# Cross attention blocks: a later row turn, a spread start, and plain fp32 projections in the first layer

## Chip, cores and metric

One core of one Trainium2 chip. The metric is device time in microseconds of the whole kernel (two transformer layers). TensorE is called PE, VectorE DVE, ScalarE ACT, GpSimd POOL and SyncE SP, as in the profile.

## The reference, cut to what matters

Both layers do self attention, cross attention and a feed forward part. x is (4, 1024, 256) in float32 and the context (4, 77, 192); 16 heads, of width 16 in the first layer ("narrow", its weights fake-quantised) and 64 in the second ("wide"). The change touches the cross attention alone:

```
h    = layernorm(x) * g + b                      # rows of 256
q    = (h @ wq).reshape(b, n, 16, HD)            # HD = 16, then 64
sim  = einsum(q, k) * HD ** -0.5                 # k, v from the 77 context rows
out  = einsum(softmax(sim), v).reshape(b, n, 16 * HD)
x    = x + out @ wo + bo
```

## The kernel before

x stays in SBUF through the whole kernel. Each layer calls `context_kv` (keys and values of the context, stored to DRAM), `norm_project` and `attend_...` (self attention), `cross_block` (L2097), and `feed_forward`. Phases are separated by a barrier.

`cross_block` cuts the 4096 rows into 8 tiles of 512 (TT; TB = 4 blocks of 128) and the 16 heads into 8 pairs: 64 slots n = 8 t + p. Every engine has its own loop over n, written out in full, and runs its instructions strictly in that order; semaphores tie them together. In slot n:

- PE (L2457 on): `score(n)` (waits until DVE has read score n-1), the queries due in this slot (`query`), `values(n - 3)`, a piece of the output projection (`project`, four per tile, in slots 7, 8, 11 and 12 from the tile's start), `flip(n - 2)` (transposes of the probabilities), and, if a later tile is due, `turn` (transposes of the normalised rows, L2465).
- DVE (L2319): maximum and subtraction of score n, sum and reciprocal n - 1, the addition of a projected piece to x, `low_query` and `low_out` (the low parts), then for a later tile the statistics, `turn_rows` (normalised rows xhat, L2322) and `low_rows` (L2331).
- ACT (L2396): exp, `high_query`, `high_out` (evictions rounded to the high part), `scale` (gain and offset of the turned rows, L2399), and the copy of the flipped probabilities.
- POOL (L2275): the reciprocal deviations (`norm_rstd`), the bias added to x, the division of the probabilities; before the loop zeroing of buffers and low parts of both weights.
- SP (L2209): all DMAs. In the narrow block `stack(t)` stores the q of a tile to DRAM and loads it back as three parts stacked on partitions; `score` waits for that (`moved`).

A matmul of near fp32 accuracy is made of three float32r passes: high x high, low x high and high x low, with every operand split into a high part (ACT copy to float32r) and a low part (the rest, DVE or POOL). `turn_of(n)` names the tile whose rows are normalised in slot n. LEAD and TURN_AT set it: narrow (2, 5), so tile t in slot 8 (t - 2) + 5; wide (1, 1), so in slot 8 (t - 1) + 1. Statistics come three slots earlier, POOL's deviations two; PE turns in the same slot as `turn_rows`, ACT scales one slot later, `low_rows` two later. Queries of tile t are due from slot 8 (t - 1) + 1 on (narrow, both) and from 8 t - 2 (wide, one a slot). FIRST, the loop's first n, follows from LEAD and TURN_AT: -6 and -2. PSUM results of `turn`, `query`, `values` and `project` go round four banks in the order that `unit` counts; `clear` waits until the one four before has been evicted (`kind_sem`).

Before the loop, SP loads gains, wq, bias, then contexts (all four in the narrow block, two in the wide), and after the low part of wq is made, wo into the same raw buffer.

Of the kernel before, what the change touches and what calls it, by code (L numbers as in the profile page):

```python
# [12 lines left out]
P = 128  # L13
# [83 lines left out]
class Program:  # L97
# [1999 lines left out]
    def cross_block(self, L, x_sb, ident, g, b, wq, wo, bo):  # L2097
# [10 lines left out]
        LEAD, TURN_AT = (2, 5) if narrow else (1, 1)  # L2108
# [54 lines left out]
        with ExitStack() as st:  # L2163
# [6 lines left out]
            ht = sb("ht", [P, DC, TT])  # L2170
            h = [[sb(f"h_{part}{k}", [P, DC, TT], F32R) for k in two] for part in ("hi", "lo")]
            gam, bet = sb("g", [P, DC]), sb("b", [P, DC])
            wraw = sb("wraw", [P, 2048])
            wqr = [sb("wq_hi", [P, DC, L.dim], F32R), sb("wq_lo", [P, DC, L.dim], F32R)]
            wor = [sb("wo_hi", [P, OCH, D], F32R), sb("wo_lo", [P, OCH, D], F32R)]
# [12 lines left out]
            o = [sb("o_hi", [P, OCH, TT], F32R), sb("o_lo", [P, OCH, TT], F32R)]  # L2188
# [3 lines left out]
            gb_in, w_in, b_in, w_hi, w_lo, zeroed = (sem(s) for s in ("gb_in", "w_in", "b_in", "w_hi", "w_lo", "zeroed"))  # L2192
# [11 lines left out]
            ZERO = KVB * 2  # L2204
            WOL = 16 * (G if narrow else 1)
            kind_sem = dict(tp=hh_done, q=q_lo, acc=o_lo, y=y_done)

            @block.sync
            def _(sp):  # L2209
# [24 lines left out]
                raw = wraw[:, 0:DC * L.dim].rearrange("p (c n) -> p c n", c=DC)  # L2234
                sp.dma_start(raw, wq.rearrange("(c p) n -> p c n", p=P)).then_inc(w_in, 16)
                sp.dma_start(bias[:, :], bo.partition_broadcast(P)).then_inc(b_in, 16)
                for bt in range(KVB):
                    sp.wait_ge(zeroed, 2 * bt + 2)
                    context(bt)
                sp.wait_ge(w_lo, 1)  # L2240
                if narrow:
                    sp.wait_ge(zeroed, ZERO + 1)
                    raw = wraw[:, 0:OCH * D].rearrange("p (c n) -> p c n", c=OCH)
                    view = wo.rearrange("(c h e) n -> h e c n", h=G, e=HD)
                    for x in range(G):
                        sp.dma_start(raw[W * x:W * x + HD, :, :], view[x]).then_inc(w_in, 16)
                else:
                    raw = wraw[:, 0:OCH * D].rearrange("p (c n) -> p c n", c=OCH)
                    sp.dma_start(raw, wo.rearrange("(c p) n -> p c n", p=P)).then_inc(w_in, 16)
# [25 lines left out]
            def _(pool):  # L2275
# [14 lines left out]
                size = DC * L.dim  # L2290
                pool.wait_ge(w_hi, 1)
                lo, hi = (wqr[x][:, :, :].rearrange("p c n -> p (c n)") for x in (1, 0))
                g_.tensor_tensor(lo, wraw[:, 0:size], hi.bitcast(F32), ALU.subtract).then_inc(w_lo, 1)
                for k in range(1, KVB):
                    zero(k)
                if narrow:
                    pool.wait_ge(w_lo, 1)
                    g_.memset(wraw[:, 0:OCH * D], 0.0).then_inc(zeroed, 1)
                pool.wait_ge(w_hi, 2)
                lo, hi = (wor[x][:, :, :].rearrange("p c n -> p (c n)") for x in (1, 0))  # L2300
                g_.tensor_tensor(lo, wraw[:, 0:OCH * D], hi.bitcast(F32), ALU.subtract).then_inc(w_lo, 1)
                pool.wait_ge(b_in, 16)
                for n in range(FIRST, SLOTS):
# [5 lines left out]
                    if p == 0:  # L2309
                        pool.wait_ge(n_["chain"], (t + 1) * self.STATS_STEPS)  # L2310
                        xt = x_sb[:, t * TB:(t + 1) * TB, :]
                        g_.tensor_tensor(xt, xt, bias[:, :].unsqueeze(1).broadcast_to((P, TB, D)), ALU.add).then_inc(biased, 1)
# [3 lines left out]
                                     .broadcast_to((P, 2 * TB, M)), ALU.mult).then_inc(p_norm, 1)  # L2316

            @block.vector
            def _(dve):  # L2319
# [42 lines left out]
                low_rows(0)  # L2362
                for c in range(QCH if narrow else 2):
                    low_query(0, c)
                for n in range(FIRST, LAST):
# [20 lines left out]
                    if acc_of(n - 3):  # L2386
# [5 lines left out]
                    if turn_of(n - 2):  # L2392
                        low_rows(turn_of(n - 2))

            @block.scalar
            def _(act):  # L2396
                a_ = nc.scalar

                def scale(t):  # L2399
                    for c in range(DC):  # L2400
                        act.wait_ge(r_ready, at["tp", t, c] + 1)
                    if t > 0:
                        act.wait_ge(hl_done, t)
                    for c in range(DC):
                        a_.activation(ht[:, c, :], bank[at["tp", t, c] % 4][:, :], ACT.Identity, bias=bet[:, c:c + 1],
                                      scale=gam[:, c:c + 1]).then_inc(ht_done, 1)
# [24 lines left out]
                act.wait_ge(w_in, 16)  # L2431
                a_.activation(wqr[0][:, :, :].rearrange("p c n -> p (c n)"), wraw[:, 0:DC * L.dim], ACT.Copy).then_inc(w_hi, 1)
# [3 lines left out]
                act.wait_ge(w_in, 16 + WOL)  # L2436
                a_.activation(wor[0][:, :, :].rearrange("p c n -> p (c n)"), wraw[:, 0:OCH * D], ACT.Copy).then_inc(w_hi, 1)
# [346 lines left out]
```

## Time and profile before

| | us |
|---|---|
| median of 3 runs (lowest, highest) | 4611.16 (4599.38, 4611.64) |
| profiled execution, its own time | 4588.91 |
| its span | 4586.7 |
| PE busy | 4023.8 (88%) |
| DVE busy | 3057.8 (67%) |
| ACT busy | 1795.5 (39%) |
| POOL busy | 1774.3 (39%) |

The spans are those of one execution; busy times are shares of it over all phases. A matmul's duration holds its latency, so the distance from one start to the next tells its price. Clock is the TensorE clock that was granted, as a share of 2.4 GHz; its lower level is 0.5.

### The profile page before, as it was taken

The numbers are of one execution on the slowest core, as the hardware profiler recorded it, in microseconds if no ns is written. First come the engines' busy times: TensorE is split into PE (matmuls) and PEld (weight loads), VectorE is DVE, ScalarE is ACT, GpSimd is POOL, SyncE is SP. The second block draws the span as 40 slices with busy tenths as digits, with TensorE's granted clock in tenths as the row PEclk, the third lists the DMA queues.
The fourth block names the chain that finished last, engine by engine and source line by source line (L and its number), as shares of the span: only waits on it lengthen the run. The fifth ranks groups of instructions, "written<-read, shape, count | busy, mean of one in ns | idle before, by whom it ended". The sixth has DMA issues, their size and how long they took to land. (4 is left out here: it accounts for less than half of the span.)

```text
span 4586.7 us, 67259 instructions
## 1 busy us (share of the span) xinstructions
PE 4023.8 (88%) x25111; PEld 2701.5 (59%) x25111; DVE 3057.8 (67%) x4993; ACT 1795.5 (39%) x2644; POOL 1774.3 (39%) x1164
## 2 busy tenths in 40 slices
PE   0779999995787897699899999999999979999798
PEld 0633333332565676477566666666666647777677
DVE  6768888882676655477567666666666646665565
ACT  0226676764444332111233333333333324444332
POOL 0168800001333000100377877787787762222000
PEclk9859999998788999799799999999999989889899
DMA  4453443421432000577411111111121110000100
GB/s 117 168 88 53 61 40 34 47 20 35 72 62 44 20 0 20 165 279 283 144 70 47 68 49 57 60 48 69 47 70 47 47 37 1 9 9 1 34 15 18
DMA packets 303482, 293.18 MB, mean 64 GB/s; under 512 B 132340, under 2 KB 222612, under 8 KB 302924
## 3 DMA queue, kind: packets, MB, share of 16 engines
q1 hardware_dynamic: 300620, 281.27, 24.0%
q0 software_dynamic: 2560, 7.88, 0.6%
q8 instruction: 191, 3.13, 0.3%
q14 instruction: 111, 0.91, 0.1%
HBM read 160.74 MB, written 127.28 MB: 63 GB/s over the span
## 5 line engine op out<-in xcount | busy, mean ns | idle before, releaser
L1704 POOL TENSOR_TENSOR f_sums<-f_sums,f_probs 128x1024 f32<-128x1024 f32 x384 | 914.3, 2381 | 156.0 <-ACT f_probs L1823 118.1
L1721 DVE TENSOR_REDUCE f_mx<-f_s 128x1 f32<-128x512 f32 x1024 | 660.0, 687 | 383.8 <-PE f_s L1846 372.5
L1823 ACT ACTIVATE f_probs<-f_st 128x1024 f32<-128x1024 f32 x512 | 525.1, 1027 | 939.7 <-PE f_st L1869 935.3
L1327 DVE TENSOR_REDUCE f_mx<-f_s 128x1 f32<-128x512 f32 x1024 | 633.4, 683 | 94.7 <-PE f_s L1464 83.3
L1440 ACT ACTIVATE f_probs<-f_st 128x512 f32<-128x512 f32 x1024 | 530.2, 603 | 252.1 <-PE f_st L1481 251.0
L1846 PE MATMUL f_s<-f_k,f_q 64*128 64x512 f32 x3072 | 516.0, 415 | 21.7 <-DMA f_k<-k 15.6
L1869 PE MATMUL f_st<-f_q,f_k 64*128 64x512 f32 x3072 | 485.9, 390 | 1.1 <-ACT f_probs L1823 1.0
L1883 PE MATMUL f_acc<-f_probs,f_v 128*64 128x512 f32 x2048 | 465.4, 596 | 0.0
L1846 PEld LDWEIGHTS f_s<-f_k,f_q 64*128 64x128 f32 x3072 | 341.9, 189 | 169.8 <-issue 115.2
L1481 PE MATMUL f_st<-f_q,f_k 50*128 50x512 f32 x1024 | 354.7, 485 | 58.3 <-ACT f_probs L1440 58.2
L1869 PEld LDWEIGHTS f_st<-f_q,f_k 64*128 64x128 f32 x3072 | 367.3, 184 | 25.8 <-ACT f_probs L1823 3.8
L2315 POOL TENSOR_TENSOR f_probs<-f_probs,f_rden 128x616 f32<-128x616 f32 x128 | 160.3, 1253 | 550.3 <-DVE f_rden L2381 550.3
L1481 PEld LDWEIGHTS f_st<-f_q,f_k 50*128 50x128 f32 x1024 | 143.4, 189 | 361.2 <-ACT f_probs L1440 312.0
L1464 PE MATMUL f_s<-f_k,f_q 48*128 48x512 f32 x1024 | 317.7, 459 | 22.9 <-DMA f_k<-k 22.6
L576 POOL TENSOR_TENSOR f_ve<-f_var,f_const 128x4 f32<-128x4 f32 x48 | 9.6, 199 | 788.6 <-DVE f_var L557 788.6
L1883 PEld LDWEIGHTS f_acc<-f_probs,f_v 128*64 128x64 f32 x2048 | 141.5, 137 | 266.2 <-issue 257.2
L1493 PE MATMUL f_acc<-f_probs,f_v 128*32 128x512 f32 x2048 | 281.0, 622 | 0.0
L1744 DVE RECIPROCAL f_rd<-f_s 128x512 f32<-128x512 f32 x64 | 214.9, 3358 | 72.4 <-PE f_s L1892 72.4
L1869 PE MATMUL f_st<-f_m,f_mones 64*128 64x512 f32 x1024 | 248.4, 389 | 0.0
L2369 DVE TENSOR_REDUCE f_mx<-f_s 128x8 f32<-128x616 f32 x128 | 101.9, 796 | 207.3 <-PE f_s L2506 206.6
L2634 DVE SCALAR_TENSOR_TENSOR f_u<-f_pa,f_bias,f_gate 128x512 f32<-128x512 f32 x128 | 96.1, 751 | 213.5 <-PE f_pa L2720 213.4
L2671 ACT ACTIVATE f_gate<-f_pg,f_bias 128x512 f32<-128x512 f32 x128 | 88.0, 687 | 380.7 <-PE f_pg L2712 380.7
(258 smaller groups left out, 8334.0 us busy)
## 6 DMA issues: line engine op xcount, KB each, us to landing
q<-f_stage SPq DMA_DIRECT2D x80, 512.0 KB, 2.8
k<-f_stage SPq DMA_DIRECT2D x80, 512.0 KB, 2.8
f_q<-q SPq DMA_DIRECT2D x32, 1024.0 KB, 5.0
f_k<-k SPq DMA_DIRECT2D x32, 1024.0 KB, 7.4
v<-f_v_stage SPq DMA_DIRECT2D x64, 256.0 KB, 3.1
f_v<-v SPq DMA_DIRECT2D x32, 512.0 KB, 8.5
f_q<-q SPq DMA_DIRECT2D x96, 128.0 KB, 4.3
f_k<-k SPq DMA_DIRECT2D x96, 128.0 KB, 7.0
```

What stands on the lines that cost most here:

```text
L1327: v.tensor_reduce(mx[:, i % 2, c:c + 1], bank[u % 4][:, :], AX_X, ALU.max).then_inc(s_free, 1)
L1440: a_.activation(probs[:, n % NP, e % 2, :], stb[k % 3][:, :], ACT.Exp, scale=L.scale).then_inc(p_ready, 1)
L1464: t.matmul(bank[u % 4][:, :], q[cur][rows, j, qb * P:(qb + 1) * P], k_[cur][rows, j, f * HALF:(f + 1) * HALF], start=True, stop=True, tile ...
L1481: t.matmul(stb[n % 3][:, :], k_[cur][rows, j, c * P:(c + 1) * P], q[cur][rows, j, half * HALF:(half + 1) * HALF], start=True, stop=True, t ...
L1493: ins = t.matmul(acc[W * h:W * h + W, :], vs[cur][:, c, h, :], p, start=c == 0, stop=c == KC - 1, tile_position=(0, W * h))
L1704: g_.tensor_tensor(out, out, probs[:, n % NP, :, :], ALU.add).then_inc(sum_done, 1)
L1721: v.tensor_reduce(mx[:, i % 2, c:c + 1], bank[u % 3][:, :], AX_X, ALU.max).then_inc(s_free, 1)
L1744: v.reciprocal(rd[:, half, :], bank[u % 3][:, :]).then_inc(s_free, 1)
L1823: a_.activation(probs[:, s % NP, :, :], stb[s % 2][:, :, :], ACT.Exp, scale=L.scale).then_inc(p_ready, 1)
L1846: ins = t.matmul(bank[u % 3][:, :], q[cur][rows, a, qb * P:(qb + 1) * P], k_[cur][rows, c, f * HALF:(f + 1) * HALF], start=r == 0, stop=r ...
L1869: ins = t.matmul(stb[s % 2][:, h, :], lhs, rhs, start=r == 0, stop=r == 3, tile_position=(64 * h, 0))
L1883: ins = t.matmul(acc[W * h:W * h + W, :], vs[cur][:, c, h, :], probs[:, s % NP, h, :], start=c == 0, stop=c == KC - 1, tile_position=(0, W ...
```

## The change

`turn` follows `turn_rows` by one slot, and `scale` and `low_rows` follow it; the wide block has LEAD 2 and TURN_AT 4, so tile t's rows are normalised in slot 8 (t - 2) + 4 and turned in the next, and FIRST becomes -7. The narrow block keeps plain fp32 h, wq, o and wo: no high and low parts of these four, one matmul for three. (Its q is still split for `stack`.) wo has a raw buffer and a semaphore of its own. SP issues one context, then wo and the bias; further contexts come between the tiles' stacks (narrow) or after (wide). POOL zeroes later context buffers in slots 1 to 3, makes wo's low part in slot 3 (wide), and adds the bias in slot 4 of a tile, not 0.

```diff
-        LEAD, TURN_AT = (2, 5) if narrow else (1, 1)
+        LEAD, TURN_AT = 2, 5 if narrow else 4
...
-            if turn_of(n):
+            if turn_of(n - 1):
                 for c in range(DC):
-                    unit("tp", turn_of(n), c)
+                    unit("tp", turn_of(n - 1), c)
...
+            if narrow:
+                h = [[sb(f"h{k}", [P, DC, TT]) for k in two]]
+            else:
+                ht = sb("ht", [P, DC, TT])
+                h = [[sb(f"h_{part}{k}", [P, DC, TT], F32R) for k in two] for part in ("hi", "lo")]
...
+            wraw, oraw = sb("wraw", [P, DC * L.dim]), sb("oraw", [P, OCH * D])
+            if narrow:
+                wqr, wor = [wraw[:, :].rearrange("p (c n) -> p c n", c=DC)], [oraw[:, :].rearrange("p (c n) -> p c n", c=OCH)]
...
-            o = [sb("o_hi", [P, OCH, TT], F32R), sb("o_lo", [P, OCH, TT], F32R)]
+            o = [sb("o", [P, OCH, TT])] if narrow else [sb("o_hi", [P, OCH, TT], F32R), sb("o_lo", [P, OCH, TT], F32R)]
...
-            kind_sem = dict(tp=hh_done, q=q_lo, acc=o_lo, y=y_done)
+            kind_sem = dict(tp=hh_done, q=q_lo, acc=o_hi if narrow else o_lo, y=y_done)
... SP
-                sp.dma_start(bias[:, :], bo.partition_broadcast(P)).then_inc(b_in, 16)
-                for bt in range(KVB):
-                    sp.wait_ge(zeroed, 2 * bt + 2)
-                    context(bt)
-                sp.wait_ge(w_lo, 1)
+                sp.wait_ge(zeroed, 2)
+                context(0)
+                raw = oraw[:, :].rearrange("p (c n) -> p c n", c=OCH)
                 if narrow:
-                    sp.wait_ge(zeroed, ZERO + 1)
+                    sp.wait_ge(o_zeroed, 1)
...
+                sp.dma_start(bias[:, :], bo.partition_broadcast(P)).then_inc(b_in, 16)
...
                 if narrow:
                     for t in range(TILES):
                         stack(t)
+                        if t + 1 < KVB:
+                            sp.wait_ge(zeroed, 2 * t + 4)
+                            context(t + 1)
                 else:
+                    sp.wait_ge(zeroed, 4)
+                    context(1)
... POOL
-                for k in range(1, KVB):
-                    zero(k)
...
-                    if p == 0:
-                        pool.wait_ge(n_["chain"], (t + 1) * self.STATS_STEPS)
...
                                      .broadcast_to((P, 2 * TB, M)), ALU.mult).then_inc(p_norm, 1)
+                    if 0 < n < KVB:
+                        zero(n)
+                    if n == 3 and not narrow:
+                        pool.wait_ge(w_hi, 2)
+                        lo, hi = (wor[x][:, :, :].rearrange("p c n -> p (c n)") for x in (1, 0))
+                        g_.tensor_tensor(lo, oraw[:, :], hi.bitcast(F32), ALU.subtract).then_inc(w_lo, 1)
+                    if p == 4:
+                        pool.wait_ge(b_in, 16)
+                        pool.wait_ge(n_["chain"], (t + 1) * self.STATS_STEPS)
+                        xt = x_sb[:, t * TB:(t + 1) * TB, :]
+                        g_.tensor_tensor(xt, xt, bias[:, :].unsqueeze(1).broadcast_to((P, TB, D)), ALU.add).then_inc(biased, 1)
... DVE
-                    if acc_of(n - 3):
+                    if acc_of(n - 3) and not narrow:
                         low_out(*acc_of(n - 3))
...
-                    if turn_of(n - 2):
-                        low_rows(turn_of(n - 2))
+                    if turn_of(n - 3) and not narrow:
+                        low_rows(turn_of(n - 3))
... ACT
+                    if n == 2 and not narrow:
+                        act.wait_ge(wo_in, WOL)
+                        a_.activation(wor[0][:, :, :].rearrange("p c n -> p (c n)"), oraw[:, :], ACT.Copy).then_inc(w_hi, 1)
...
-                    if turn_of(n - 1):
-                        scale(turn_of(n - 1))
+                    if turn_of(n - 2):
+                        scale(turn_of(n - 2))
... PE
+                    passes = [(k, 0, 0) for k in range(DC)] if narrow else self.H_PASSES
...
-                    pe.wait_ge(o_lo, nth("acc", t, part * half + half - 1))
-                    pe.wait_ge(w_lo, 2)
+                    pe.wait_ge(kind_sem["acc"], nth("acc", t, part * half + half - 1))
...
-                        work = [(c, x, w) for c in range(part * half, part * half + half) for x, w in ((0, 0), (0, 1), (1, 0))]
+                        work = [(c, x, w) for c in range(part * half, part * half + half) for x, w in (((0, 0),) if narrow else ((0, 0), (0, 1), (1, 0)))]
...
-                    if turn_of(n):
-                        turn(turn_of(n))
+                    if turn_of(n - 1):
+                        turn(turn_of(n - 1))
```

## Rows read from the trace of the kernel before

**Rows 1.** Windows, narrow tiles 0, 1, 6: length, busy PE, PEld, DVE, ACT, POOL; clock
```profile
1155.52:1195.48 39.96, 31.64 (x160) 23.70 (x160) 26.98 (x49) 15.91 (x22) 11.61 (x14) 0.55 0.38 66
1195.48:1236.81 41.33, 33.58 (x228) 26.02 (x228) 30.87 (x57) 19.15 (x27) 15.08 (x16) 0.79 0.39 64
...
1400.83:1431.28 30.45, 25.91 (x220) 19.72 (x220) 25.85 (x43) 16.71 (x23) 11.82 (x10) 1.00 0.53 87
```

**Rows 2.** Windows, wide tiles 0, 3, 6
```profile
3762.91:3816.37 53.46, 43.69 (x335) 33.34 (x336) 34.90 (x60) 22.71 (x32) 19.68 (x23) 0.81 0.01 4
...
3940.67:4002.12 61.45, 59.36 (x441) 44.58 (x442) 36.83 (x67) 24.69 (x36) 14.24 (x16) 0.89 0.01 1
...
4124.71:4181.84 57.13, 54.74 (x441) 41.47 (x442) 34.89 (x57) 24.55 (x36) 12.08 (x9) 0.97 0.01 1
```

**Rows 3.** Groups by line, 1154 to 1475 (narrow): busy, mean ns, idle before
```profile
L2349 DVE TENSOR_TENSOR f_o_lo<-f_r,f_o_hi 128x512 fp32r<-128x512 f32 x32 | 22.0, 688 | 14.1 <-ACT f_o_hi L2428 14.1
...
L2471 PE MATMUL f_r<-ident,f_xhat 128*128 128x128 f32 x48 | 10.7, 396 | 19.6 <-DVE f_xhat L2328 19.6
...
L2405 ACT ACTIVATE f_ht<-f_r,f_b,f_g 128x512 f32<-128x512 f32 x12 | 8.6, 775 | 0.0
...
L2336 DVE TENSOR_TENSOR f_h_lo<-f_ht,f_h_hi 128x1024 fp32r<-128x1024 f32 x6 | 8.2, 1366 | 0.3 <-PE f_r L2541 0.3
```

**Rows 4.** Groups by line, 3759 to 4245 (wide)
```profile
L2471 PE MATMUL f_r<-ident,f_xhat 128*128 128x128 f32 x56 | 9.4, 321 | 20.4 <-DVE f_xhat L2328 20.4
```

**Rows 5.** Timeline of PE, wide tile 3: start, duration, instruction, idle before
```profile
3954.23 1.09 PE L2471 MATMUL f_r<-ident,f_xhat 128*128 128x128 f32 x8 [2.09 <-DVE f_xhat L2328]
```

**Rows 6.** Windows of PE after it: length, PE busy, clock
```profile
3956.00:3958.00 2.00, 2.00 (x17) 0.52 0.00 0
...
3968.00:3970.00 2.00, 2.00 (x6) 0.56 0.00 0
```

**Rows 7.** Timeline of PE, wide tile 6, a slot after its turn
```profile
4147.85 0.47 PE L2480 MATMUL f_r<-f_h_hi,f_wq_hi 128*128 128x512 f32 x1 [0.31 <-ACT f_h_hi L2410]
```

**Rows 8.** Timeline, start of the wide block
```profile
3746.27 1.38 DVE L2328 TENSOR_SCALAR f_xhat<-x_rows,f_mean,f_rstd 128x256 f32<-128x256 f32 x4 [2.88 <-POOL f_rstd L588]
...
3760.78 1.40 DVE L545 BATCH_NORM_STATS2 f_stats<-x_rows 128x6 f32<-128x256 f32 x4
...
3762.91 0.79 DVE L2369 TENSOR_REDUCE f_mx<-f_s 128x8 f32<-128x616 f32 x1
```

**Rows 9.** Timeline, start of the narrow block
```profile
1106.95 1.85 SPq L2218 DMA_DIRECT2D f_ks<-ckh  x4
...
1107.40 0.20 POOL L576 TENSOR_TENSOR f_ve<-f_var,f_const 128x4 f32<-128x4 f32 x1 [0.98 <-DVE f_var L557]
...
1109.79 3.53 SPq L2227 DMA_DIRECT2D f_v<-cv  x4
...
1110.14 3.80 DVE L2328 TENSOR_SCALAR f_xhat<-x_rows,f_mean,f_rstd 128x256 f32<-128x256 f32 x4 [2.89 <-POOL f_rstd L588]
...
1126.46 0.69 DVE L2343 TENSOR_TENSOR f_q_lo<-f_r,f_q_hi 128x512 fp32r<-128x512 f32 x1 [1.87 <-ACT f_q_hi L2421]
...
1134.16 0.43 SPq L2256 DMA_DIRECT2D q<-f_q_hi  x1
...
1138.47 2.72 SPq L2264 DMA_DIRECT2D f_qs<-q  x6
...
1154.40 1.08 PE L2506 MATMUL f_s<-f_ks,f_qs 48*128 48x78 f32 x8 [6.67 <-DMA f_qs<-q]
```

**Rows 10.** Timeline of PE at full clock: two query passes, values narrow, values wide
```profile
1200.78 0.39 PE L2480 MATMUL f_r<-f_h_hi,f_wq_hi 128*128 128x512 f32 x1
1201.01 0.40 PE L2480 MATMUL f_r<-f_h_lo,f_wq_hi 128*128 128x512 f32 x1
...
1205.02 1.06 PE L2528 MATMUL f_r<-f_probs_t,f_v 77*32 77x512 f32 x8 [0.54 <-ACT f_probs_t L2454]
...
3942.15 1.08 PE L2528 MATMUL f_r<-f_probs_t,f_v 77*64 77x512 f32 x4
```

More of the change, by code:

```diff
@@ L2289, in _ @@
                 self.norm_rstd(pool, n_, 0)
[L2290 to L2293, printed above, removed]
-                for k in range(1, KVB):
-                    zero(k)
-                if narrow:
[L2297 to L2302, printed above, removed]
+                if narrow:
+                    g_.memset(oraw[:, :], 0.0).then_inc(o_zeroed, 1)
+                else:
+                    pool.wait_ge(w_hi, 1)
+                    lo, hi = (wqr[x][:, :, :].rearrange("p c n -> p (c n)") for x in (1, 0))
+                    g_.tensor_tensor(lo, wraw[:, :], hi.bitcast(F32), ALU.subtract).then_inc(w_lo, 1)
                 for n in range(FIRST, SLOTS):
@@ L2361, in _ @@
                 turn_rows(0)
-                low_rows(0)
+                if not narrow:
+                    low_rows(0)
                 for c in range(QCH if narrow else 2):
@@ L2401, in scale @@
                         act.wait_ge(r_ready, at["tp", t, c] + 1)
[L2402 to L2406, printed above, removed]
+                    if not narrow:
+                        if t > 0:
+                            act.wait_ge(hl_done, t)
+                        for c in range(DC):
+                            a_.activation(ht[:, c, :], bank[at["tp", t, c] % 4][:, :], ACT.Identity, bias=bet[:, c:c + 1],
+                                          scale=gam[:, c:c + 1]).then_inc(ht_done, 1)
                     if t >= 2:
@@ L2430, in _ @@
                 act.wait_ge(gb_in, 32)
-                act.wait_ge(w_in, 16)
-                a_.activation(wqr[0][:, :, :].rearrange("p c n -> p (c n)"), wraw[:, 0:DC * L.dim], ACT.Copy).then_inc(w_hi, 1)
+                if not narrow:
+                    act.wait_ge(w_in, 16)
+                    a_.activation(wqr[0][:, :, :].rearrange("p c n -> p (c n)"), wraw[:, :], ACT.Copy).then_inc(w_hi, 1)
                 scale(0)
@@ L2476, in query @@
                     pe.wait_ge(hh_done, DC * (t + 1))
-                    pe.wait_ge(hl_done, t + 1)
+                    if not narrow:
+                        pe.wait_ge(hl_done, t + 1)
                     clear(u)
-                    for j, (k, a, bb) in enumerate(self.H_PASSES):
+                    passes = [(k, 0, 0) for k in range(DC)] if narrow else self.H_PASSES
+                    for j, (k, a, bb) in enumerate(passes):
                         ins = t_.matmul(bank[u % 4][:, :], wqr[a][:, k, c * P:(c + 1) * P], h[bb][t % 2][:, k, :],
-                                        start=j == 0, stop=j == len(self.H_PASSES) - 1)
+                                        start=j == 0, stop=j == len(passes) - 1)
                     ins.then_inc(r_ready, 1)
@@ L2545, in _ @@
                 turn(0)
-                pe.wait_ge(w_hi, 1)
-                pe.wait_ge(w_lo, 1)
+                if narrow:
+                    pe.wait_ge(w_in, 16)
+                else:
+                    pe.wait_ge(w_hi, 1)
+                    pe.wait_ge(w_lo, 1)
                 for c in range(QCH if narrow else 2):
```

28 lines of the change are left out of this document (12 added, 16 removed).

## The prediction

> **What bounds the kernel now.** I looked first at which stretches the diff can reach. Only the two cross attention blocks are touched: the first layer's (narrow, about 1105 to 1475 us) and the second's (wide, about 3741 to 4250 us), together a fifth of the span of 4586.7 us. Each runs 64 slots (8 row tiles of 8 head pairs), and since everything is written in a fixed order per engine, I then cut both blocks into tiles with the windows view, from the first maximum of a tile to that of the next. What the reader is to see:
>
> Narrow: a tile in the middle takes 41.33 us although PE is busy only 33.58 and DVE 30.87, at a granted clock of 0.79. Tile 6 takes 30.45 at clock 1.00 [rows 1]. It differs by one thing: no rows of a later tile are normalised and turned in it. So a turn costs nearly 11 us, of which PE's own transposes are a small part.
>
> Wide: PE is the bound (59.36 busy of 61.45), and still the tile runs at clock 0.89; tile 6, which has a turn too, takes 57.13 at 0.97 [rows 2].
>
> The lines view says what PE waits for at the turn: the eight transposes of `turn` stand behind `turn_rows` of DVE in the same slot, 19.6 us over 6 turns in the narrow block (3.3 each) and 20.4 us over 7 in the wide one [rows 3, 4], 2.09 of them in wide tile 3 [rows 5]. The fine windows show the rest of the price: within two to four us of that wait the clock goes to its lower level (1.2 GHz), and stays there until about 3969 [rows 6]. With 0.89 as the mean of 0.5 and 1, 22% of the tile, 13.5 us, ran at half clock and lost 6.8 us.
>
> **The change part by part.**
>
> 1) *Turn a slot later, wide tiles.* DVE now normalises in slot 4 and PE turns at the end of slot 5, which is a whole slot of PE work later; DVE has 36.83 busy of 61.45, so the rows are there. Wide tile now: 61.45 - 2.1 (wait) - 6.8 (half clock) = 52.6. What is late next: ACT. `scale` issues four evictions, and the copy of the turned probabilities stands behind them; in tile 6, which is nearly at full clock, PE already waited 0.31 for it [rows 7]. As some 3 us before that were still at half clock, which gave ACT about 1.5 us, I allow 1.6 us (ends 0.3 and 2). So 54.2, gain 7.2 in each of tiles 1 to 5: 36. Tile 6 no longer has any turn: 57.13 less the wait 2.1, ACT's 0.3, transposes 1.0 and 1.7 for the 3% of missing clock is 52.0, gain 5.1. Tile 7 stays. The biases of POOL, moved to p == 4, come after the division of the slot, DVE needs them three slots later: nothing.
>
> 2) *Wide start.* LEAD 2 puts the statistics, rows, turn and scaling of tile 1 between the first queries and score 0, on each engine's order. In the trace tile 1's statistics begin at 3760.78 and the first maximum is at 3762.91 [rows 8]. Now: statistics 2.2, POOL's seven small steps 2.7 (1107.40 to 1110.14 [rows 9]), rows 1.4 [rows 8], turn at half clock 2.0 (twice the 1.09 of [rows 5]), ACT's four evictions 3.0 (0.775 each), `low_rows` 1.4 [rows 3], and DVE reaches the maximum at about 3773.5: 10.6 late. In return tile 0 (53.46 [rows 2]) loses the turn in slot 1, the wait for it and ACT's and POOL's wait for the output weights, which arrive early now; eight slots of about 5.6 (52.0 / 8 is a full slot's 6.5, and its first slots have no values and no project yet) give about 44.6. Net +1.7. Wide together: -36 - 5 + 2 = -39.
>
> 3) *Narrow start.* Today the chain is: rows 1110.14 (3.80, beside a POOL subtraction and memsets), turn, ht and h_hi on ACT, h_lo, queries, q_lo ending 1127.15, and then nothing until 1134.16, because SP still issues three more contexts and the output weights. From the first store of q to score 0 it is 20.24 us, to the second store's landing 4.3, then 15.9 of loads [rows 9]. After: the rows stand beside one memset, I take 1.9 instead of 3.80 (alone they take 1.38 [rows 8]); no ht (-1.5), no h_lo (-1.4, both [rows 3]). The queries are 4 fp32 matmuls, at half clock 7.2 instead of 5.6 (part 4): q_lo ends at 1127.15 - 1.9 - 1.5 - 1.4 + 1.6 = 1124.0 and SP is free. 1124.0 + 20.2 = 1144.2: 10.1 earlier.
>
> 4) *fp32 instead of high and low parts.* PE: six passes of 512 columns, 0.233 apart at full clock, are 1.40 per query unit; a project unit is 12 of half the columns, 1.41 likewise [rows 10]. The nearest fp32 row is the values matmul: 4 source matmuls of 32 output rows take 8 records and 1.06 us, 2 of 64 rows take 4 records and 1.08 [rows 10]. Time did not change with half the records, so the column groups run at once and one fp32 matmul of 512 columns is two records and 0.85 to 1.0 us. A query unit (2 of them) is 1.7 to 2.0, a project unit (4 of 256 columns) the same; I take 1.8, as weights of the next one load under the matmul. That adds 0.4 x (2 + 4) = 2.4 us per tile to PE (1.8 to 3.6); nothing hides it when PE is last. Bounds from both sides: 0 if the records pack better than these rows, 3.6.
>
> The Trainium skill, "FP8 and Floating Point Precision", section TensorE Precision Notes, speaks against this part: a true FP32 matmul makes four passes through the array, where three reduced ones were used. By it the 48 units would cost 4/3 of 1.4, 22 us more in the block, where my sum from the rows has 0.4 x 48 = 19; the trace agrees with it as far as the two values rows go.
>
> DVE loses `low_out` (22.0 / 32 x 4 = 2.75 per tile) and `low_rows` (8.2 / 6 = 1.37) [rows 3], ACT two evictions per turn. PE's project no longer waits for o_lo.
>
> 5) *Narrow tiles.* At full clock tile 6 has PE 25.91 and DVE 25.85 in 30.45 [rows 1]: two engines that hand slots to each other lose 4.5 over the longer one. After, a turn tile has PE 25.9 + 2.4 + 1.0 = 29.3, DVE 30.87 - 4.1 = 26.8, so 33.8 against 41.33: -7.5 in tiles 1 to 5, -37.5. Tile 6: +1.5, tile 7: +1.5 (PE longer, DVE shorter). Tile 0 (39.96, clock 0.55) saves the wait of 3.3 and pays about that for longer queries at half clock: 0. POOL's zeroing of later contexts now sits between divisions, 1.2 us in a POOL that is busy 15 of 41: nothing.
>
> 6) *SP's order.* In the loop the second context is issued before `stack(1)` and waits for POOL's zeroing in slot 1. One context is 6.4 us of issue (1106.95 to 1113.32 [rows 9]). Zeroed about 16 us into tile 0, issued until 23, then 20.2 to landing: 43 us, against a tile 0 of 40. I put +2 (0 to 10). Later tiles: q ready at 10.5, landing at 31, needed at 34: just enough.
>
> Narrow together: -10 - 37.5 + 3 + 2 = -42. Sum -81: the profiled execution, 4588.91 us (span 4586.7 and 2.2 around it), becomes 4508. The median of the runs shown is 22 us above that execution (4611.16), so the forecast as a median is 4611 - 81 = 4530.
>
> **The rivals.**
>
> A, *the clock falls anyway.* The waits of 1 to 2 us that the new order leaves on PE (ACT's copy behind `scale`; in the narrow block the statistics in slot 2) also bring it down once per tile. Then wide tiles stay near 61 (54.2 + 6.8) and narrow ones come to about 38: only the start, 2.8 x 5 and tile 6 are won: -20 to -25, 4588. For it: 0.79 over 41.33 us is 17 us at half clock per narrow tile, more than the one wait at the turn brought in the wide block. Against: tile 6 of both blocks holds 0.97 to 1.00 with waits up to 1 us.
>
> B, *the loads are late.* If the narrow tiles come to less than 32 us, or the second stack is 8 us late, the loads (20 us after q_lo) take PE's place: +10 to +15, 4543.
>
> C, *slower: fp32 in a block that stays at half clock.* Place: the narrow slots, PE. Tile 0 ran at 0.55 through with PE busy 31.64 of 39.96, so a busy PE does not by itself bring the clock up. At half clock throughout a tile's PE work is 2 x 29.3 = 58.6: +17 in five tiles, +25 in each of the last two, less 10 at the start: +125, less the wide 39: 4697. It outweighs the wide gain once a narrow tile takes over 47 us, with a mean clock under about 0.62. The fp32 passes cost double there, and no DVE saving helps.
>
> D, *the wait moves.* DVE's rows are still late, behind POOL's bias (now in the same slot as the narrow rows), or the turn waits for a freed bank; gain only at the starts, with the fp32 cost: within 10 us of before, 4605.
>
> **How the numbers follow.** The forecast has 0.58 (own range 4505 to 4560), A 0.17, B 0.12, C 0.06, D 0.07. What this kernel's measurement can tell from no change is about 0.3%, 14 us. Faster: the forecast, A nearly whole, B: 0.87. Same: most of D, a little of A: 0.07. Slower: C and an edge of D, 0.06. The range reaches up to A, 4588, and down to 4490, where narrow tiles come to 31 us, fp32 costs nothing and ACT's wait is 0.3.
>
> **What would show it.** The wait of `turn` on `xhat` gone in both blocks. Wide tiles 1 to 5 at 53 to 55 us with clock 0.97 or more; narrow ones at 33 to 36 with 0.9. First narrow score 36 to 38 us after POOL's first small step instead of 47. Query and project matmuls in pairs of records, 1.7 to 2.0 us a unit. Wide first maximum some 10 us later after the block's start. Wrong, if wide tiles keep a clock near 0.89 (A), if score waits for `qs` in several tiles (B), or if narrow clock is below 0.65 (C).

## The result, and the profile after

The changed kernel takes 4558.02 us (median of 4 runs, 4539.39 to 4574.30) where the kernel before, in the same comparison, takes 4611.4 (4599.38 to 4615.29). The ratio is 0.9887 with an interval of 0.9845 to 0.9929: faster by 1.1%, 53 us, of the 81 that were forecast. Its profiled execution took 4539.39 us (span 4537.6); that of before took 4588.91 (span 4586.7). The two differ by 49 us, and the account below is made between them.

Busy time of the whole program, from the page of the changed kernel:

```profile
PE 4003.8 (88%) x24951; PEld 2664.9 (59%) x24951; DVE 3035.7 (67%) x4953; ACT 1778.9 (39%) x2626; POOL 1763.4 (39%) x1162
```

Each block is now read from its own first statistics, since the phases ahead of the narrow block, whose code is the same, came out 4.28 us longer in this execution (first statistics at 1109.31 instead of 1105.03). From there the blocks split into the stretches that the prediction used. Windows of the changed kernel, from first maximum to first maximum: narrow tiles 0, 1, 2 and 6, then wide tiles 0, 3 and 6 (stretch, length, busy time and instructions of PE, PEld, DVE, ACT, POOL, clock, DMA share, GB/s):

```profile
1147.80:1189.02 41.22, 28.78 (x156) 19.60 (x160) 26.40 (x47) 15.01 (x20) 16.26 (x21) 0.67 0.53 80
1189.02:1229.63 40.61, 35.75 (x208) 24.74 (x208) 29.15 (x53) 17.36 (x24) 14.20 (x16) 0.80 0.49 73
1229.63:1270.04 40.41, 33.66 (x208) 23.76 (x208) 29.01 (x52) 18.15 (x25) 14.20 (x16) 0.87 0.39 65
...
1386.63:1420.89 34.26, 30.96 (x200) 21.87 (x200) 23.66 (x38) 16.60 (x23) 11.99 (x9) 0.90 0.48 78
...
3766.23:3813.37 47.14, 42.97 (x339) 30.73 (x338) 35.81 (x60) 22.38 (x32) 18.72 (x18) 0.91 0.10 21
...
3920.22:3973.75 53.53, 53.08 (x441) 40.49 (x442) 36.74 (x68) 24.11 (x36) 14.23 (x16) 1.00 0.01 1
...
4080.88:4133.05 52.17, 52.17 (x433) 39.62 (x434) 32.29 (x53) 21.67 (x32) 12.07 (x9) 1.00 0.00 1
```

These stand against [rows 1, 2]. With the tiles between, which are read the same way:

| stretch | before | after | difference | forecast |
|---|---|---|---|---|
| narrow, to the first maximum | 50.49 | 38.49 | -12.0 | -10.1 |
| narrow tile 0 | 39.96 | 41.22 | +1.3 | +2 (with the late stack) |
| **narrow tiles 1 to 5** | 205.4 | 197.6 | **-7.7** | **-37.5** |
| narrow tile 6 and tile 7, to its last maximum | 58.9 | 64.7 | +5.9 | +3 |
| wide, to the first maximum | 21.74 | 32.34 | +10.6 | +10.6 |
| wide tile 0 | 53.46 | 47.14 | -6.3 | -8.9 |
| wide tiles 1 to 5 | 308.3 | 267.5 | -40.8 | -36 |
| wide tile 6 | 57.13 | 52.17 | -5.0 | -5.1 |

Narrow -12.6, wide -41.6, the phases before +4.3, the rest +0.8: -49. One term is missing, the narrow tiles 1 to 5. In the wide block PE is busy almost without a gap (53.08 of 53.53 us) and at clock 1.00, where it had 0.89. The narrow tiles still take 38.1 to 40.6 us, where they took 40.6 to 41.3, and their clock only went from 0.79 to 0.83 up to 0.80 to 0.87.

Two of the smaller terms depend on the execution. With the same code in it, wide tile 0 takes 47 us at clock 0.91 in six profiled executions (after and experiments 2, 3, 7, 8 and 9) and 53 to 55 us at 0.75 to 0.79 in three (1, 6 and 10). Narrow tile 6 takes 34.3 us at 0.90 here, and 30.7 and 31.3 at 1.00 in experiments 4 and 5, which have the same narrow code.

What narrow tile 2 waits for, from the timeline of the changed kernel (start, duration, instruction, idle before):

```profile
1247.59 1.07 PE L2542 MATMUL f_r<-f_probs_t,f_v 77*32 77x512 f32 x8 [1.02 <-ACT f_probs_t L2466]
...
1256.82 3.94 DVE L2336 TENSOR_SCALAR f_xhat<-x_rows,f_mean,f_rstd 128x256 f32<-128x256 f32 x4
...
1257.56 2.39 POOL L2324 TENSOR_TENSOR x_rows<-x_rows,f_bias 128x1024 f32<-128x1024 f32 x1
...
1260.81 1.09 PE L2483 MATMUL f_r<-ident,f_xhat 128*128 128x128 f32 x8 [1.63 <-DVE f_xhat L2336]
...
1263.59 3.78 PE L2558 MATMUL f_r<-f_oraw,f_o 128*128 128x256 f32 x8 [0.59 <-ACT f_o L2438]
```

The wait of the turn on `xhat` has not gone. It is 1.63 us here, where its mean was 3.3 [rows 3], and that although the turn comes a slot later. The normalisation takes 3.94 us and runs beside POOL's addition of the output bias, which the change moved to the same slot. The project unit behind the turn takes 3.78 us, twice its length at full clock. The windows of PE alone over that place (stretch, length, PE busy, clock, DMA share, GB/s) say so directly:

```profile
1259.00:1261.00 2.00, 0.37 (x4) 1.00 0.00 0
1261.00:1263.00 2.00, 1.54 (x16) 0.99 0.00 0
1263.00:1265.00 2.00, 1.42 (x3) 0.50 0.00 0
...
1267.00:1269.00 2.00, 2.00 (x9) 0.50 0.00 0
```

This is the pattern of [rows 5, 6]: a wait, then some two us after its end the lower level of 1.2 GHz.

The two largest waits of PE in narrow tiles 1 to 5, from the waits view of the changed kernel (who waited for whom, total us, times, longest):

```profile
PE f_r L2542 <- ACT f_probs_t L2466: 14.3, 19, 1.0
PE f_r L2483 <- DVE f_xhat L2336: 7.2, 5, 1.6
```

The largest sum is not the turn's but that of the copy on ACT. It stood there before the change as well (10.5 us over the same five tiles, the turn 16.9), and the prediction did not price it here.

The start of the narrow block in the changed kernel's timeline answers to [rows 9]:

```profile
1114.42 1.96 DVE L2336 TENSOR_SCALAR f_xhat<-x_rows,f_mean,f_rstd 128x256 f32<-128x256 f32 x4 [2.90 <-POOL f_rstd L588]
...
1120.12 5.10 PE L2494 MATMUL f_r<-f_h,f_wraw 128*128 128x512 f32 x8 [1.71 <-ACT f_h L2420]
...
1125.88 0.69 DVE L2351 TENSOR_TENSOR f_q_lo<-f_r,f_q_hi 128x512 fp32r<-128x512 f32 x1 [1.02 <-ACT f_q_hi L2431]
...
1126.60 0.40 SPq L2259 DMA_DIRECT2D q<-f_q_hi  x1
...
1130.85 2.71 SPq L2267 DMA_DIRECT2D f_qs<-q  x6
...
1146.69 1.07 PE L2520 MATMUL f_s<-f_ks,f_qs 48*128 48x78 f32 x8 [11.79 <-DMA f_qs<-q]
```

`q_lo` ends at 1126.57 and the first store is issued at once: the seven us in which SP was still issuing later contexts are gone. From there to score 0 it is 20.1 us, as before (20.2).

### The profile page after: what moved, and what is told of

The parts are those of the page before. It is cut to its first block and busy times, and to the rows that moved or that the text cites. A ratio compares the mean times of both kernels' runs of the same rounds, so it can differ in the third digit from the quotient of the medians.

```text
span 4537.6 us, 66887 instructions
## 1 busy us (share of the span) xinstructions
PE 4003.8 (88%) x24951; PEld 2664.9 (59%) x24951; DVE 3035.7 (67%) x4953; ACT 1778.9 (39%) x2626; POOL 1763.4 (39%) x1162
```

## The experiments

The theory was that three things in the narrow block took the missing 30 us: POOL's bias in the slot of the normalisation, ACT's evictions ahead of the copy that PE wants, and the clock that falls after such waits. Its rivals: that the fp32 matmuls cost what the rest won, that a turn has a price wherever it stands, and, for the wide block, that the gain is the place of the turn and not the lag. The measure of each run is the sum of tiles 1 to 5 of a block, from its own profiled execution. Before: 205.4 narrow, 308.3 wide. After: 197.6 and 267.5. It repeats well where the code of the block is the same: 197.6, 198.5 and 197.7 narrow (after, experiments 4 and 5), and 266.9 to 267.7 wide in the nine profiled executions with the changed wide block. The totals of single executions don't: those of the changed kernel alone go from 4539 to 4574.

**1. POOL's bias in another slot.**

```diff
-                    if p == 4:
+                    if p == (2 if narrow else 4):
```

> Changed kernel with the narrow block's bias addition of POOL in slot 2 of a tile instead of slot 4; all else the same. Theory 1 (POOL's bias addition of 2.4 us stands beside DVE's xhat and slows it from 1.9 to 3.9 us, so the turn is still late and the clock falls after it): xhat back to about 2 us, PE's wait of 1.6 us at the turn gone, narrow tiles 1 to 5 at 33 to 37 us instead of 38.1 to 40.6, in all 10 to 25 us faster than the changed kernel's 4539.4 profiled. Rival (fp32 on PE took the gain): narrow tiles lose at most 1.5 us each, under 7 us in all.

Ratio to before 0.9859 (0.9804 to 0.9915), 4551.94 us. Narrow tiles 1 to 5 take 189.8: 42.3, 37.7, 37.6, 36.0 and 36.2. Windows of tiles 2 and 4, and the normalisation of tile 2 in the timeline:

```profile
1252.96:1290.62 37.66, 33.59 (x208) 23.90 (x208) 27.10 (x52) 17.81 (x25) 14.16 (x16) 0.86 0.42 70
...
1328.23:1364.19 35.96, 31.89 (x208) 22.72 (x208) 27.11 (x53) 16.89 (x24) 13.67 (x16) 0.91 0.46 74
```

```profile
1280.16 1.90 DVE L2336 TENSOR_SCALAR f_xhat<-x_rows,f_mean,f_rstd 128x256 f32<-128x256 f32 x4
```

The same instruction takes 1.90 us instead of 3.94, and the turn no longer waits. DVE's busy time falls by the same 2.0 (29.15 to 27.10). The gain of 7.8 us is less than the theory asked. Two lines of the waits view over these five tiles say why:

```profile
PE f_r L2542 <- ACT f_probs_t L2466: 14.9, 18, 1.4
PE f_t L2530 <- POOL f_probs L2312: 4.8, 5, 2.3
```

The line of `xhat` (7.2) is gone, and one of 4.8 has come: in slot 2 the addition delays POOL's own division of the next probabilities, for which PE waits up to 2.3 us. In slot 4 it hit DVE, in slot 2 it hits POOL. The collision is one part of the missing term, and this run removed it only in exchange for a smaller one. Experiment 7 has the same edit and gains 5.7 us in these tiles, so the exchange is worth 6 to 8.

**2. The narrow block with high and low parts again**, the order of the change kept:

```diff
+        plain = False
...
-            if narrow:
+            if plain:
                 ...                     # at each place that chooses fp32 or high and low parts
```

> Changed kernel, but the narrow block keeps the high and low parts of h, wq, o and wo with three passes each, as before; late turn and spread start stay. Rival (fp32 took the gain): tiles 1 to 5 shorter by 3 us or more each, tile 6 back from 34.3 to 30.5 and tile 7 from 30.5 to 28.4, 15 to 25 us faster in all. Theory 1: DVE gets 4.1 us per tile back, so tiles 1 to 5 stay within 1.5 us or grow; tiles 6 and 7 win 6 together, the start loses 3 to 5; total within 8 us of the changed kernel.

Ratio 0.9925 (0.9892 to 0.9958), 4578.11 us, narrow tiles 217.1, which is 19.5 more than after. The fp32 matmuls did not cost the block anything; they saved it some 4 us a tile. The window of tile 3 and, in the next, ACT's order and PE's wait:

```profile
1296.54:1340.89 44.35, 36.08 (x228) 26.69 (x228) 32.88 (x57) 19.16 (x27) 14.25 (x17) 0.77 0.37 60
```

```profile
1341.19 1.45 ACT L2421 ACTIVATE f_h_hi<-f_r,f_b,f_g 128x512 fp32r<-128x512 f32 x2
...
1342.51 1.01 ACT L2467 ACTIVATE f_probs_t<-f_t 77x1024 f32<-77x1024 f32 x1
...
1343.58 1.92 PE L2543 MATMUL f_r<-f_probs_t,f_v 77*32 77x512 f32 x8 [2.73 <-ACT f_probs_t L2467]
```

Four evictions of 0.7 us, of which the row shows the last two, stand ahead of the copy of the turned probabilities, and PE waits 2.73 us for that copy. With fp32 they are two. In this order of the instructions, what fp32 removes from ACT and DVE is on the path and what it adds to PE is not. The run also shows what the rest of the change did to the narrow tiles: with high and low parts in both, they take 217.1 us in the new order against 205.4 before, 11.7 us more. The 7.7 us that the change won in these tiles are fp32's 19.5 less the order's 11.7.

**3. Contexts 1 to 3 issued behind the stack of the same number.**

```diff
-                        if t + 1 < KVB:
-                            sp.wait_ge(zeroed, 2 * t + 4)
-                            context(t + 1)
+                        if 0 < t < KVB:
+                            sp.wait_ge(zeroed, 2 * t + 2)
+                            context(t)
```

> Changed kernel with contexts 1 to 3 issued after the stack of the same number instead of before it. If the second stack's loads are late because SP waits for POOL's zeroing and issues a context first: the 9.8 us slot at the end of narrow tile 0 goes to about 5 and tile 0 from 41.2 to about 36; 5 to 7 us faster. Rival: that slot is long because of half clock and PE work; then tile 0 stays within 1 us.

Ratio 0.9847 (0.9792 to 0.9901), 4536.49 us. Tile 0 takes 36.24 instead of 41.22. Its window, and SP's first store of `q` in it:

```profile
1149.14:1185.38 36.24, 29.13 (x152) 19.31 (x152) 26.40 (x46) 13.76 (x19) 15.76 (x21) 0.65 0.56 82
```

```profile
1159.52 0.40 SPq L2259 DMA_DIRECT2D q<-f_q_hi  x1
```

In the changed kernel the timeline shows the context ahead of the stack and the score behind it waiting:

```profile
1164.79 3.33 SPq L2233 DMA_DIRECT2D f_v<-cv  x4
...
1168.16 0.52 SPq L2259 DMA_DIRECT2D q<-f_q_hi  x1
...
1187.90 1.07 PE L2520 MATMUL f_s<-f_ks,f_qs 48*128 48x78 f32 x8 [5.57 <-DMA f_qs<-q]
```

The store of `q` comes 20.4 us after tile 0's first maximum there, and 10.4 us after it here. The wait of 5.57 us was the stack's, issued behind a context, and 5.0 us of tile 0 went with it.

**4. The wide turn in the slot of its rows**, slot 4, with no lag:

```diff
+        LAG = 0 if not narrow else 1
...
-                    if turn_of(n - 1):
-                        turn(turn_of(n - 1))
+                    if turn_of(n - LAG):
+                        turn(turn_of(n - LAG))
                 ...                     # scale, low_rows and the banks' order shifted alike
```

> Changed kernel, but in the wide block the turn is issued in the slot of its rows again (slot 4), scale and low parts one and two slots later; LEAD 2 stays. If the lag of a slot is what removed the wait: PE waits about 2 us again at each turn, the clock comes back to 0.89 and wide tiles 1 to 5 to 60 us or more, about 35 us slower. Rival (the slot chosen does it: slot 4 holds a project piece, 8 us of PE work, in which DVE gets done): wait under 0.5 us, tiles at 53 to 55, total within 5 us.

Ratio 0.9909 (0.9878 to 0.9940), 4566.44 us. The wide tiles 1 to 5 take 277.7: four of them about 55 at clock 1.00, and tile 4 57.7 at 0.94. The window of tile 1:

```profile
3828.77:3883.69 54.92, 52.85 (x441) 40.28 (x442) 36.71 (x67) 24.33 (x36) 14.24 (x16) 1.00 0.01 1
```

So the lag is worth 2.0 us a tile ((277.7 - 267.5) / 5) and the move from slot 1 to slot 4 6.1 ((308.3 - 277.7) / 5). In slot 4 PE has a project piece ahead of the turn, in which DVE gets the rows done; slot 1 has none. The move to slot 4 also holds LEAD 2 and POOL's bias in slot 4 instead of 0, which no run separates; DVE's rows take 1.37 to 1.38 us in both places. The wait on `xhat` is gone either way, so that the first expectation (60 us or more) fails, and its rival (53 to 55) is nearly right but for tile 4. What is left, in tiles 1 to 5, is a wait for a bank (waits view; then the wait in tile 4 and PE's clock behind it):

```profile
PE f_r L2543 <- DVE x_rows L2367: 8.8, 5, 1.8
...
4031.93 1.08 PE L2543 MATMUL f_r<-f_probs_t,f_v 77*64 77x512 f32 x4 [1.77 <-DVE x_rows L2367]
...
4034.00:4036.00 2.00, 2.00 (x20) 0.50 0.00 0
```

The same wait of 1.8 us stands in each of the five tiles. Behind it the clock stayed at 1.00 in four and fell to 0.50 for some 7 us in one. For the clock, the length of the wait alone doesn't decide.

**5. The wide lag alone**, rows in slot 1 and turn in slot 2:

```diff
-        LEAD, TURN_AT = 2, 5 if narrow else 4
+        LEAD, TURN_AT = (2, 5) if narrow else (1, 1)
```

> Changed kernel, but the wide block keeps LEAD 1 and TURN_AT 1 of before: rows in slot 1, turn in slot 2 (the lag alone). If the lag by itself takes the wait and the clock loss away, as the prediction had it: wide tiles 1 to 5 at 53.5 to 55 us and clock 1.00, the first maximum about 10 us earlier in the block. Rival (the lag is worth only the 1.5 us that the kernel with the same slot lost, and slots 4 and 5 did the rest, because project pieces stand there): tiles at 57 us or more with a clock below 0.95.

Ratio 0.9942 (0.9918 to 0.9967), 4581.39 us, wide tiles 288.4, 57.3 to 58.4 each. The window of one, the wait inside it, and PE's clock behind it:

```profile
3889.24:3946.87 57.63, 54.67 (x441) 42.07 (x442) 36.55 (x67) 24.23 (x36) 14.24 (x16) 0.97 0.08 18
```

```profile
3913.78 0.36 PE L2558 MATMUL f_r<-f_wo_hi,f_o_hi 128*128 128x256 f32 x1 [2.96 <-ACT f_h_hi L2420]
```

```profile
3914.00:3916.00 2.00, 2.00 (x12) 0.57 0.00 0
```

The wait on `xhat` goes here too, and another takes its place: the next project piece needs the bank that holds the turned rows, which is free only when ACT has made `h_hi`, 2.96 us late. The lag alone gives 4 us a tile, the slot alone gives 6.1, both give 8.2 (308.3 less 267.5, over five). The time is the rival's (57 or more), and the clock, 0.97 in four tiles and 0.94 in one, lies mostly between the two expectations.

**6. The narrow turn in the slot of its rows**, slot 5, with fp32; the edit is that of experiment 4 with `LAG = 0 if narrow else 1`.

> Changed kernel, but in the narrow block the turn is issued in the slot of its rows (5) and scaled one slot later; fp32 operands and spread start stay. If the lag pays in the narrow block too: PE waits 3 to 5 us at each turn again, tiles 1 to 5 at 42 to 45 us, 12 to 25 us slower than the changed kernel's tiles (197.6 us in sum). Rival (POOL's bias and the clock have taken the lag's gain already): tiles within 1 us of the changed kernel's 38 to 40.6.

Ratio 0.9968 (0.9937 to 0.9998), 4590.93 us, narrow tiles 221.9: 44.4 each. Window and turn of one:

```profile
1278.82:1323.20 44.38, 35.95 (x208) 25.14 (x208) 29.22 (x53) 17.80 (x25) 14.21 (x16) 0.81 0.36 60
```

```profile
1309.99 1.97 PE L2484 MATMUL f_r<-ident,f_xhat 128*128 128x128 f32 x8 [5.40 <-DVE f_xhat L2337]
```

Without the lag, PE waits 5.40 us for the rows. The narrow lag is worth 4.9 us a tile beside POOL's bias, more than twice the 2.0 of the wide block in slot 4. The bias explains about 2 us of the difference to before: the rows take 3.92 us in this run and took 1.90 before, where the wait was 3.4 at most. That a narrow slot has less PE work in which DVE can catch up is likely the rest; no run shows it. Without the lag the tile is slower than the 41.33 of before [rows 1].

**7. Edits 1 and 3 together.**

> Bias in slot 2 (narrow) and contexts after the stack of the same number, together. If they are two separate costs: tile 0 at 36 us, tiles 1 to 5 at 36 to 38 (sum 186), total 15 us under the changed kernel. Rival: the earlier tiles make the loads of the next stack late, and one takes from the other: no more than 8 us.

Ratio 0.9853 (0.9809 to 0.9897), 4539.09 us; tile 0 38.0, narrow tiles 191.9 (41.9, 36.0, 36.2, 36.7, 41.1). It is between the two alone and not below them. The same instructions take 36 us in three tiles and 41 in two; their clocks are 0.91, 0.95 and 0.91, and 0.80 and 0.83. The gains did not add up, and what sets the clock back in the first and the fifth is open; PE's wait for POOL's division, 8.1 us in these five tiles, is larger here than in experiment 1.

**8. The narrow turn at slot 3**, the bias left in slot 4, the contexts as in experiment 3:

```diff
-        LEAD, TURN_AT = 2, 5 if narrow else 4
+        LEAD, TURN_AT = 2, 3 if narrow else 4
```

> Contexts later as before, and the narrow block with TURN_AT 3: statistics in slot 0, rows in slot 3 beside a project piece, turn in slot 4, bias of POOL still in slot 4 and so behind the rows. If what remains in the narrow tiles is DVE's extra work standing in slots where PE has little (2 and 5) and the clock that falls in these: xhat 2 us, tiles 1 to 5 at 32 to 35 us, sum 160 to 175, clock 0.95 or more, 25 to 35 us under the changed kernel. Rival (the fall of the clock comes from PE's short waits for ACT's copies whatever the slot): tiles at 36 to 38, clock under 0.9.

Ratio 0.9855 (0.9815 to 0.9895), 4539.08 us; narrow tiles 187.7, 37.5 each. The rows are free of the bias here. Window of a tile and the wait in it:

```profile
1260.30:1297.84 37.54, 32.87 (x208) 22.99 (x208) 27.54 (x53) 18.13 (x25) 14.24 (x16) 0.86 0.43 71
```

```profile
1287.43 1.94 PE L2542 MATMUL f_r<-f_probs_t,f_v 77*32 77x512 f32 x8 [2.35 <-ACT f_probs_t L2466]
```

The time and the clock are the rival's (36 to 38, under 0.9). The wait has moved to ACT. The copy of the probabilities stands behind `scale`, PE loses 2.35 us, and the values behind it run at half clock (1.94 us against 1.06 in [rows 10]).

**9. The same, with ACT's scaling behind the copy.**

```diff
-                    if turn_of(n - 2):
+                    if turn_of(n - 2) and not narrow:
                         scale(turn_of(n - 2))
                 ...                     # the copy of the turned probabilities
+                    if turn_of(n - 2) and narrow:
+                        scale(turn_of(n - 2))
```

> The kernel with TURN_AT 3 and contexts later, with ACT's scaling of the turned rows issued behind its copy of the probabilities in the narrow block. There PE waited 2.35 us in slot 6 for that copy and the clock fell. If that wait behind the scaling is what is left over in the narrow tiles: wait in slot 6 about 0.5 us, clock 0.95 or more, tiles 1 to 5 at 32 to 34.5 us instead of 37.5 (15 to 27 us in sum). Rival (the clock falls anyway from PE being idle in the light slots 5 and 6): tiles at 36.5 or more.

Ratio 0.9838 (0.9801 to 0.9875), 4526.23 us, the lowest median of all. Narrow tiles take 178.5, by turns 35.1 and 36.6, and tile 0 34.1. Windows of tiles 1 and 2, and the place of the wait:

```profile
1192.47:1227.56 35.09, 31.74 (x208) 22.55 (x208) 27.55 (x53) 18.03 (x25) 14.77 (x17) 0.90 0.58 85
1227.56:1264.20 36.64, 33.30 (x208) 23.32 (x208) 27.54 (x52) 18.03 (x25) 14.26 (x16) 0.86 0.52 81
```

```profile
1253.36 1.94 PE L2544 MATMUL f_r<-f_probs_t,f_v 77*32 77x512 f32 x8 [1.02 <-ACT f_probs_t L2466]
```

PE's waits in these five tiles:

```profile
PE f_r L2544 <- ACT f_probs_t L2466: 13.2, 20, 1.0
PE f_s L2522 <- DVE f_probs L2382: 3.5, 5, 0.7
```

The copy's total is 13.2 us where experiment 8 had 19.8, and the waits on `xhat` and on POOL are both gone. Two lines of order are worth 9.2 us here (187.7 to 178.5), less than the 15 to 27 that were expected; the time lies between the two expectations. Behind the wait of 1.02 us the values run at half clock at once (1.94 us; the clock from 1252 to 1254 is 0.79), so the clock fell in that wait or just before it, and not two us after it as in the changed kernel. In the profiles this version is 19 us below after in tiles 1 to 5 and 7 in tile 0. The intervals of the two ratios overlap (0.9801 to 0.9875 and 0.9845 to 0.9929), so that it beats the changed kernel is likely, not shown by the times alone.

**10. Edit 9's order with turn and bias as in experiment 7** (turn at slot 5, bias at slot 2).

> Rows still in slot 5 (as in the changed kernel), bias in slot 2, contexts later, scaling behind the copy. If the scaling ahead of the copy is the remaining cost here too: tiles 1 to 5 at 34 to 35 us, clock 0.95. Rival (here the fall comes in slot 4 after the statistics of slot 2, which the order on ACT doesn't touch): tiles within 1 us of the 36 to 37.7 with the bias alone moved.

Ratio 0.9868 (0.9837 to 0.9900), 4545.18 us; narrow tiles 183.1: 38.6, 37.6, 36.0, 35.5, 35.4. Against experiment 7 it is 8.8 us less in the tiles, but 9.0 of that lie in the two tiles whose clock was low there; the other three are within 1.6 us either way. Against experiment 1, with the contexts still early, it is 6.7 us less, of which 3.7 lie in tile 1, which ran at clock 0.76 there. PE still waits 6.4 us for POOL's division, behind the bias at slot 2, which experiment 9 avoids. At slot 5 the order on ACT by itself is not shown to give much; at slot 3 it gave 9. Tiles 4 and 5 reach clock 0.95 here, and still take 35.4 us.

## Why the prediction was right, and where its size was off

Direction and range held (4558 in 4490 to 4588), and 53 of 81 us came. That 4558 lies in the forecast's own range too, which ended at 4560, says little for its mechanism: the narrow tiles came out where rival A had put them. By its steps:

- **1) The wide turn a slot later.** Right in size, -40.8 for -36, with PE at clock 1.00 and no wait on `xhat`. Half right in its reason: it credited the slot of lag. Experiments 4 and 5 show that slot 4 alone, beside a project piece, gives 6.1 us a tile, the lag alone 4.0 with a new wait for a bank, and both 8.2. Of the 1.6 us that were allowed for ACT in each tile, PE's wait for `h_hi` shows 0.5 (2.3 over five tiles).
- **2) The wide start.** +10.6 was forecast and came (+10.2 to +11.4 in the other executions of the same code). Tile 0 was forecast at 44.6 and took 47.14, still partly at the lower clock (0.91); as said above, it can take 55. The collision of step 5 is in it too: DVE's rows take 5.39 us beside POOL's low part of wo (4.54 us), and the turn waits 0.85 us for them.
- **3) The narrow start.** -12.0 for -10.1. The chain was right link by link, rows 1.96 for 1.9 and 20.1 us from `q_lo` to score 0 for 20.2. The queries took 5.1 us and not 7.2, since the clock rose while they ran (0.50 before 1122, 1.00 from 1124 on).
- **4) fp32 units.** Two query units of tile 2 take 3.70 us at clock 1.00 in the timeline of the changed kernel, 1.85 each for the 1.8 that was taken:

```profile
1234.49 3.70 PE L2494 MATMUL f_r<-f_h,f_wraw 128*128 128x512 f32 x8
```

  The price of fp32 can be read where tile 6, which has no turn, runs at full clock with fp32 too, in the window of experiment 4:

```profile
1409.12:1439.85 30.73, 27.77 (x200) 19.34 (x200) 23.67 (x39) 16.23 (x23) 11.57 (x9) 1.00 0.54 87
```

  PE is 1.9 us longer than in tile 6 of [rows 1] and DVE 2.2 shorter, and the tile grows by 0.3 us. The sign of the whole part was taken from PE's side, while experiment 2 shows that in tiles with a turn the path runs over DVE and ACT, and that going back costs 19.5 us.
- **5) Narrow tiles. This is the term that failed**: -37.5 forecast, -7.7 measured. Three readings went into the 33.8 us, and each was off. First, the biases of POOL "moved to p == 4 ... DVE needs them three slots later: nothing". That was argued for the wide tile, where the rows keep 1.37 us after the change, since the bias starts 7.4 us behind them. In the narrow tile the two run together: rows 3.94 us instead of 1.90, a wait of 1.63, and 6 to 8 us over five tiles by experiments 1 and 7, which still had a share of the bias to pay on POOL. What was priced was when the result is needed, and not what the instruction does to its neighbour while it runs. The Trainium skill, "SBUF — State Buffer", section SBUF: two separate sides, states that VectorE (in a two-port mode or with two inputs) and GpSimd share one port pair as an exclusive lock, where the one that comes second waits for the other's whole instruction. The trace agrees: POOL's addition takes 2.39 us, and of the 20 instructions of the rows in tiles 1 to 5 the shortest takes 0.40 us and the longest 2.44 (shortest, median and longest in ns, from the view of the tile `xhat`; which mode they run in is not shown):

```profile
L2336 DVE TENSOR_SCALAR f_xhat<-x_rows,f_mean,f_rstd x20: 400/668/2439, 1216.7 to 1377.2; 128x256 f32<-128x256 f32 x20
```

  Second, ACT's scaling ahead of the copy was priced for the wide tile and left out for the narrow one. With the turn at slot 3 it costs 9.2 us (experiments 8 and 9). In the changed kernel, with the turn at slot 5, its own share is not shown: PE's longest wait for the copy is 1.0 us there and 1.0 in experiment 9. Third, the tile was built from tile 6 at full clock. Yet no narrow tile with a turn held clock 1.00 in the traces; the best had 0.95. Tiles at 0.86 to 0.90 take 35.1 to 36.6 us in experiment 9, 1.3 to 2.8 above the 33.8. And even at 0.95 experiment 10 has 35.4: the waits for the copy of the probabilities, 2.1 us a tile or more in every version (2.9 in the changed kernel), are part of a tile with a turn. Experiment 9 brings back 19.1 of the missing 29.8 us by moving the rows away from the bias and the scaling behind the copy; the other 11 are the clock and the copy, and stay open.
- **6) SP's order.** The late stack was in the forecast with +2 (0 to 10), and the wait was 5.57, worth 5.0 (experiment 3). The forecast named cause and bounds, and chose too low. Tile 0 came to +1.3 because other things in it became shorter: without the late stack it takes 36.24 (experiment 3), 3.7 less than before.

Of the rivals, A (the clock falls anyway) was right for the narrow block, which it put at about 38 us a tile (38.1 to 40.6 came), and wrong for the wide one. D named the collision with the bias and gave it 0.07. The two blocks deserved separate chances. C did not happen: no narrow tile of the changed kernel had a mean clock under 0.67, and fp32 was no cost there. The +5.9 of tiles 6 and 7, for +3, holds the 3 to 3.5 us that the lower clock took in tile 6 of this execution.

**Open:** what brings the clock down once per narrow tile in experiment 9, where the longest wait of PE is 1.0 us. In four of experiment 4's wide tiles a wait of 1.8 us left it at 1.00 and in the fifth it did not, while 1.02 (experiment 9) and 1.63 (after) stood by a fall to 0.5. Wait length alone does not tell the cases apart. The narrow PE is less busy (31.74 of 35.09) than the wide one, which may be the difference between the blocks, but no run changed that alone, and it doesn't explain the one wide tile.

## What to carry to other kernels

When an instruction is moved to where its result is early enough, look at what runs beside it at its new place. Here an addition on POOL doubled the time of a normalisation on DVE, and that one was on the path. When a wait of the fast engine is removed, list what else that engine waits for in the same stretch, the copies on the eviction engine above all: each small wait can cost a stretch at half clock, so removing one of three brings little of its price back. And a turn wants a slot in which the bounding engine has independent work ahead of it: in the wide block that choice alone gave 6.1 us a tile and the slot of lag alone 4.0, while in the narrow block the lag gave 4.9.

## What the runs showed of the hardware

- The normalisation of 128 x 1024 fp32 in 4 instructions on DVE takes 1.38 us alone [rows 8], 1.90 to 2.25 beside a shorter piece of POOL's work (a division of 1.2 us, a memset of 1.0), 3.94 beside POOL's addition of 128 x 1024 (2.39 us), and 5.39 beside POOL's subtraction of 128 x 2048 (4.54 us).
- The output bias moved on POOL cost another engine's time in two places: in slot 4 DVE's rows of slot 5 took twice as long, in slot 2 POOL's division came up to 2.3 us late for PE. With the rows in slot 3 and the bias in slot 4 (experiments 8 and 9) PE waits for neither.
- Clock of PE: waits of 2.09 us in the wide block before [rows 5], of 2.96 in experiment 5 and of 1.63 in the narrow block after were followed by the lower level; of five waits of 1.8 us in experiment 4's wide tiles, all in the same place of the code, one was and four were not.
- An fp32 matmul of 128 rows shows as two records in the trace. Eight records of 512 columns (four matmuls) take 3.70 us at full clock; eight of 256 columns take 3.78 us at half clock.
- The same code ahead of the narrow block ended between 1105 and 1152 us in the profiled executions of the runs here (1105.03 before, 1109.31 after, 1152.11 in experiment 6). Differences of some 10 us between totals of single executions say nothing about a block; each block was therefore read from its own first statistics.
